# Eight gathers of 127 to 32 rows and eight single-row loads added at the turn between two graph layers

## The chip, the cores and the metric

The kernel runs on one core of a Trainium2 chip. The metric is the device time of one execution in microseconds (us); less is better. The core has a tensor engine (PE), a vector engine (DVE, VectorE), a scalar engine (ACT, ScalarE), GpSimd (POOL) and SyncE (SP). Each runs its own list of instructions, and they wait for each other on semaphores. Transfers between memory and the on-chip buffers are done by 16 DMA engines; SP, ACT and POOL issue them.

## The reference, cut to what matters

Two graph convolution layers over 6250 nodes with 128 features and 100000 edges, sorted by destination, then a layer norm over the features:

```python
def _cgconv(x, src, dst, edge_attr, Wf, bf, Ws, bs, gamma, beta, rmean, rvar):
    z = jnp.concatenate([x[dst], x[src], edge_attr], axis=-1)
    msg = jax.nn.sigmoid(z @ Wf + bf) * jax.nn.softplus(z @ Ws + bs)
    summed = jax.ops.segment_sum(msg, dst, num_segments=n)
    cnt = jax.ops.segment_sum(jnp.ones((dst.shape[0],), x.dtype), dst, num_segments=n)
    out = summed / jnp.maximum(cnt, 1.0)[:, None]
    out = (out - rmean) * jax.lax.rsqrt(rvar + BN_EPS) * gamma + beta
    return out + x
x1 = _cgconv(x, ...layer 1...)
x2 = _cgconv(x1, ...layer 2...)
return _layernorm(x + x2, axis=-1)
```

## The kernel before, in words

`graph_layer` (line 69) is built twice, for layer 1 and layer 2, and `finish` (line 846) adds up and normalises. Between the two layers all engines meet.

**Tables.** The part of z @ W that comes from x[src] is made once per node: PE multiplies the node features (held with the features in the partitions) by the source half of the weights, ACT copies the result out of PSUM (`stage_double`, line 510), and SP stores it in memory as `s_dram`, 6400 rows of 256 numbers of 4 bytes, in 13 stores of up to 512 KB (`store_s`, line 264; `store_rows`, line 200). The profile calls them s_rows. Layer 1 has its own table, s_dram1, and layer 2 has s_dram2.

**Steps.** The edges are worked in steps of 512 (4 tiles of 128 edges), 196 steps per layer, in 49 groups of 4 steps; 7 groups make the body of a loop. For each step POOL issues four indirect DMAs (`gather`, line 342), one per tile: each fetches 128 rows of the table, by the source index of each edge, into `pre`, a ring of 7 slots of 4 tiles. The indices lie in `ends`, which SP loads per group (`load_ends`, line 207). PE makes the rest of the product, DVE adds the two (line 716), ACT and DVE make sigmoid and softplus, and PE and DVE add the messages to a window of 64 nodes in `sums`. POOL may write a slot again when the softplus of the step 7 before is done (semaphore `s_soft`, line 378).

The first 7 steps of a layer are "plain": POOL gathers the node features themselves (rows of 128 numbers, from x or x1) and PE multiplies them, since the table isn't stored yet. For layer 2 these rows are in memory as `x1_rows`, which the profile calls x_rows.

**The turn.** At the start of layer 2, SP stores the edge counts and loads them in another shape, DVE inverts them, SP stores the inverses and loads them again, broadcast to 128 partitions, in five pieces (line 232). For each of five pieces DVE scales the sums (line 665) and adds them to x (line 668); that is the new x1 and raises `x_ready`. PE then turns x1 (line 415) and makes the table (line 395), ACT copies both (lines 531 and 516), and SP stores the 13 pieces of x1_rows of up to 256 KB (line 283) and the 13 pieces of the table (line 202) in an order written out by hand. Before these SP loads the edge ends of the first three groups (line 269) and the plan with the first edges (`read_plan`, line 252).

POOL's list at the turn is short: for each piece it waits for `x_ready` and clears that part of `sums` (memset, line 360), then it waits for all the stores of x1_rows (`rows_out`, line 361), then for the edge ends of group 0, and gathers. The memsets raise `zeroed`; DVE waits for all five (line 673) before it reads its column numbers and copies its first columns (line 834). In layer 2 the plain rows of x1 are staged in slots 0 to 4 of `pre` before they are stored; slots 5 and 6 are free until their first gather.

**The end of layer 1.** SP's last loop body issues the last loads of edges (line 250), then it waits for its own loads (lines 313 to 316) and for the other engines. The plan row `sp_tab`, which SP reads into registers with `entries` (line 236), holds ten numbers: the block of this row, eight window starts and the block of the next row.

Of the kernel before, what the change touches and what calls it, by code (L numbers as in the profile page):

```python
# [20 lines left out]
F2 = 2 * F  # L21
# [5 lines left out]
WIN = 64  # L27
# [20 lines left out]
NPAD = 6400  # L48
# [20 lines left out]
def graph_layer(nc, t, d, layer):  # L69
    first = layer == 1  # L70
    with nc.cleanup_on_exit(), ExitStack() as ctx:
        sb = lambda name, shape, dt: ctx.enter_context(nc.sbuf_tensor(f"{name}{layer}", shape, dt))
        ps = lambda name, shape, dt: ctx.enter_context(nc.psum_tensor(f"{name}{layer}", shape, dt))
        sem = lambda name: nc.alloc_semaphore(f"{name}{layer}")
# [3 lines left out]
        ends = sb("ends", [P, BODY, GTILES, 2], I32)  # L78
# [5 lines left out]
        pre = sb("pre", [P, RING, TILES, 3 * F], F32)  # L84
# [29 lines left out]
        ends_in, base_in = each("ends_in", BODY), each("base_in", BODY)  # L114
# [7 lines left out]
        s_gate, s_soft = each("gate_done"), each("soft_done")  # L122
        s_hot, s_msg, s_sum, s_added = each("hot_done"), each("msg_done"), each("sum_done"), each("added")
        passed = sem("waits_passed")
        if first:
            dsts_in, ends_of_pairs_in, bn_in = sem("dsts_in"), sem("ends_of_pairs_in"), sem("bn_in")
            iotas, cleared, gen_ready, filled = sem("iotas"), sem("cleared"), sem("gen_ready"), sem("filled")
            table_out = sem("table_out")
            flagged, totalled, plan, fast_ready = sem("flagged"), sem("totalled"), sem("plan_chain"), sem("fast_ready")
            split, bias_split = sem("bias_parts"), sem("bias_split")  # L130
            eps_added, rooted, bn_done, shifted = sem("eps_added"), sem("rooted"), sem("bn_done"), sem("shifted")
            dst_i = t["x1_t"][:, 0:ECOLS + 1].bitcast(I32)
            below = t["x1_t"][:, 2 * ECOLS:3 * ECOLS]
            bad = sb("bad", [P, 1], F32)
            pair_ends = sb("pair_ends", [1, 2, NPAIRS], I32)
            spans = sb("spans", [1, NPAIRS], F32)
            flag = sb("flag", [1, 4], F32)
            fast_rows = sb("fast_rows", [1, GROUPS + 2, ROW], I32)
            gen_rows = sb("gen_rows", [WINDOWS, GROUPS, ROW], I32)
            bn = sb("bn", [P, 2, 4], F32)  # L140
            root = sb("bn_root", [P, 2], F32)
        else:
            rows_turned, rows_staged, rows_out = sem("rows_turned"), sem("rows_staged"), sem("rows_out")
            cnt_out, cnt_in, inverted, inv_out = sem("cnt_out"), sem("cnt_in"), sem("inverted"), sem("inv_out")
            inv_in, scaled = each("inv_in", CHUNKS), sem("scaled")
            cnt = sb("cnt", [P, NPAD // P], F32)

        s_dram = t[f"s_dram{layer}"]
        plain_rows = d["x_rows"] if first else t["x1_rows"]
# [4 lines left out]
        def done(eng, sems, g, j, lag, each_inc=1):  # L154
            turns_back = (lag - j + SLOTS - 1) // SLOTS if lag > j else 0
            if isinstance(g, int):
                if g < turns_back:
                    return
                eng.wait_ge(sems[(j - lag) % SLOTS], (g - turns_back + 1) * each_inc)
            elif turns_back == 0:  # L160
                eng.wait_ge(sems[j - lag], g * each_inc + each_inc)
            else:
                eng.wait_ge(sems[(j - lag) % SLOTS], (g + (1 - turns_back)) * each_inc)
# [13 lines left out]
        def group_no(b, k):  # L177
            if isinstance(b, int):
                return b * BODY + k
            return b * BODY + k if k else b * BODY  # L180
# [8 lines left out]
        def n_bodies(eng):  # L189
            eng.wait_ge(planned, 1)  # L190
            return eng.value_load(t["choice"][:, 0:1], min_val=GROUPS // BODY - 1,
                                  max_val=GENERAL_GROUPS // BODY - 1) + 1

        def plain(b, k, j):
            return isinstance(b, int) and SLOTS * k + j < PLAIN

        def slot(k, j):
            return (SLOTS * k + j) % RING
# [7 lines left out]
        def _(sp):  # L206
# [69 lines left out]
            else:  # L276
                bodies, at = read_plan()
                stored = 0
                for c in range(CHUNKS):
                    for w in range(CUTS[c] // (4 * P), -(-CUTS[c + 1] // (4 * P))):  # L280
                        n = min(4, NPAD // P - 4 * w)
# [30 lines left out]
            groups = bodies * BODY  # L312
            sp.wait_ge(ends_in[0], bodies * 16 + 16)
            sp.wait_ge(base_in[0], bodies * 16 + 16)
            sp.wait_ge(sp_tab_in, groups * 16 + 16)
            sp.sem_inc(passed, 1)

        @block.gpsimd
        def _(pool):
            if first:  # L320
                nc.gpsimd.memset(fast_rows[:], 0).then_inc(cleared, 1)
                nc.gpsimd.iota(gen_rows[:, :, 0], [[1, GROUPS]], base=0, channel_multiplier=0).then_inc(gen_ready, 1)
                nc.gpsimd.iota(gen_rows[:, :, 1:ROW], [[0, GROUPS], [0, GPAIRS]], base=0, channel_multiplier=WIN
                               ).then_inc(gen_ready, 1)
                pool.wait_ge(cleared, 1)
                nc.gpsimd.iota(fast_rows[:, 0:GROUPS, 0], [[1, GROUPS]], base=0, channel_multiplier=0
                               ).then_inc(cleared, 1)
                nc.gpsimd.iota(t["lane"][:], [[1, WIN]], base=0, channel_multiplier=0,
                               allow_small_or_imprecise_dtypes=True).then_inc(iotas, 1)
                for q in range(PAIRS):  # L330
                    nc.gpsimd.iota(t["part"][:, q:q + 1], [[0, 1]], base=-WIN * q, channel_multiplier=1,
                                   allow_small_or_imprecise_dtypes=True).then_inc(iotas, 1)
                nc.gpsimd.memset(t["ident"][:], 0.0).then_inc(filled, 1)
                pool.wait_ge(filled, 1)
                nc.gpsimd.affine_select(out=t["ident"][:], in_=t["ident"][:], compare_op=ALU.not_equal, fill=1.0,
                                        base=0, pattern=[[-1, P]], channel_multiplier=1).then_inc(filled, 1)
                pool.wait_ge(filled, 2)
                pool.wait_ge(gen_ready, 2)
                pool.dma_start(table_rows[GENERAL_AT:GENERAL_AT + GENERAL_GROUPS, :].rearrange(
                    "(w b) c -> w b c", b=GROUPS), gen_rows[:]).then_inc(table_out, 16)  # L340

            def gather(rows, width, k, j):
                for i in range(TILES):
                    nc.gpsimd.indirect_dma_start(  # L344
                        pre[:, slot(k, j), i, 0:width], None, rows,
                        bass.IndirectOffsetOnAxis(ap=ends[:, k, j * TILES + i, 0:1], axis=0)
                    ).then_inc(src_in[k][j], 16)

            if first:
                pool.wait_ge(ends_in[0], 16)  # L350
                gather(plain_rows, F, 0, 0)
                pool.wait_ge(fast_ready, 1)
                pool.dma_start(table_rows[0:GROUPS + 1, :].rearrange("(a r) c -> a r c", a=1),
                               fast_rows[:, 0:GROUPS + 1, :]).then_inc(table_out, 16)
                pool.dma_start(table_rows[TABLE_ROWS - 2:TABLE_ROWS, :].rearrange("(a r) c -> a r c", a=1),
                               fast_rows[:, GROUPS:GROUPS + 2, :]).then_inc(table_out, 16)
            else:
                for c in range(CHUNKS):
                    pool.wait_ge(x_ready, c + 1)
                    nc.gpsimd.memset(t["sums"][:, 0, CUTS[c]:CUTS[c + 1]], 0.0).then_inc(zeroed, 1)  # L360
                pool.wait_ge(rows_out, 16 * QUADS)

            def one(b, k):
                g = group_no(b, k)
                if isinstance(b, int):
                    pool.wait_ge(ends_in[k], 16)
                else:
                    pool.wait_ge(ends_in[k], b * 16 + 16)
                pool.sem_inc(passed, 1)
                for j in range(SLOTS):  # L370
                    if plain(b, k, j):
                        if not (first and k == 0 and j == 0):
                            gather(plain_rows, F, k, j)
                        continue
                    if isinstance(b, int) and SLOTS * k + j == PLAIN:
                        for r in range(len(s_stage)):
                            pool.wait_ge(s_out[r], 16 * len(range(r, STORES, len(s_stage))))
                    done(pool, s_soft, g, j, RING)
                    pool.sem_inc(passed, 1)
                    gather(s_dram, F2, k, j)  # L380

            for k in range(BODY):
                one(0, k)
            bodies = n_bodies(pool)
            with pool.Fori(1, bodies) as b:
                for k in range(BODY):
                    one(b, k)
# [647 lines left out]
```

## Time and profile before

| | us |
|---|---|
| median of 3 runs | 2116.5 |
| lowest and highest | 2115.28 and 2119.24 |
| span of the profiled execution | 2110.8 |
| POOL, busy in the span | 1515.1 (72%) |
| VectorE | 1801.2 (85%) |
| ScalarE | 1677.5 (79%) |
| TensorE | 1557.2 (74%) |
| moved by DMA | 336.71 MB, 160 GB/s on the mean |

The profile is of one execution. The span runs from its first to its last instruction; the time of a run holds what lies around it as well, and the profiled execution's own run time is not given apart from the runs above. Layer 1 ends about 1025 us after the start of the span, layer 2's gathers run from 1065 to 2056 us, and the closing stage begins at about 2070 us. A row of the timeline gives the start, the duration, the engine with the line of the kernel, and in brackets how long the engine had been idle before and what ended that. SPq, POOLq and so on are an engine's sequencer, which issues DMAs. "DMA share" is the mean busy share of the 16 DMA engines; it can exceed 1 where packets of an engine overlap.

### The profile page before, as it was taken

The page shows a single profiled execution, that of the slowest core. Times are in us where ns is not written, and L with a number is a line of the kernel's source. Part 1 is how long each engine was busy: PE and PEld are TensorE (multiplying, and loading weights), DVE is VectorE, ACT ScalarE, POOL GpSimd, SP SyncE. Part 2 cuts the span into 40 slices and gives each one's busy share as a digit, 9 for nine tenths or more (in the row PEclk, how much of TensorE's full clock was granted, in tenths as well). Part 3 has the DMA queues.
Part 4 walks back from the last instruction along what each step waited for, and adds up shares of the span by engine and source line. Part 5 has one row for each costly group of instructions (what it writes and reads, how often), then busy time and mean ns, then how long its engine had stood idle before and what let it go on. Part 6 is the DMA issues. An engine that isn't in the chain of part 4 may idle for free. (4 is left out here: it accounts for less than half of the span.)

```text
span 2110.8 us, 35689 instructions
## 1 busy us (share of the span) xinstructions
PE 1557.2 (74%) x8321; PEld 1286.2 (61%) x8321; DVE 1801.2 (85%) x4354; ACT 1677.5 (79%) x2908; POOL 1515.1 (72%) x1589
## 2 busy tenths in 40 slices
PE   7777767767767787677487777777676776877773
PEld 6666656656556666566376666666565665665652
DVE  6899989989889898898549999898898887988887
ACT  5798888878878788788467888888787887887884
POOL 6677777777777777777267777777777777777770
PEclk9999999999999899999799999999999998999995
DMA  8455555555555555555475555555555555555542
GB/s 291 138 156 166 156 166 155 163 158 156 158 160 156 155 156 165 152 157 155 147 224 156 154 166 165 156 163 156 156 158 161 155 155 156 162 157 156 154 143 62
DMA packets 161806, 336.71 MB, mean 160 GB/s; under 512 B 58866, under 2 KB 85610, under 8 KB 161671
## 3 DMA queue, kind: packets, MB, share of 16 engines
q0 software_dynamic: 74496, 202.13, 32.5%
q1 hardware_dynamic: 85654, 131.58, 20.4%
q10 hardware_dynamic: 1522, 1.72, 0.3%
q14 instruction: 111, 0.91, 0.1%
q8 instruction: 23, 0.38, 0.1%
HBM read 315.49 MB, written 19.81 MB: 159 GB/s over the span
## 5 line engine op out<-in xcount | busy, mean ns | idle before, releaser
L344 POOL DMA_INDIRECT pre<-s_rows,ends x1512 | 1451.3, 960 | 473.8 <-issue 448.1
L458 PE MATMUL pre_ps<-rhs,lhs 128*128 128x256 f32 x3136 | 854.8, 417 | 463.5 <-DVE lhs L696 462.1
L458 PEld LDWEIGHTS pre_ps<-rhs,lhs 128*128 128x128 f32 x3136 | 607.0, 204 | 676.1 <-DVE lhs L696 385.0
L716 DVE TENSOR_TENSOR pre<-pre_ps,pre 128x1024 f32<-128x1024 f32 x378 | 460.7, 1219 | 52.6 <-DMA pre<-s_rows,ends 51.1
L548 ACT ACTIVATE pre<-pre 128x512 f32<-128x512 f32 x392 | 246.9, 630 | 309.3 <-DVE pre L716 270.0
L471 PEld LDWEIGHTS sum_ps<-hot,msg 128*128 128x128 f32 x3136 | 441.6, 204 | 53.2 <-issue 15.5
L696 DVE TENSOR_SCALAR lhs<-lhs,base_f,part 64x256 f32<-64x256 int32 x784 | 340.9, 435 | 114.2 <-issue 106.5
L471 PE MATMUL sum_ps<-hot,msg 128*128 128x64 f32 x3136 | 418.1, 279 | 24.8 <-DVE sums L736 24.8
L553 ACT ACTIVATE logs<-pre 128x1024 f32<-128x1024 f32 x392 | 414.3, 1057 | 12.4
L543 ACT COPY rhs<-dst_ps 64x256 f32<-64x256 f32 x792 | 290.0, 366 | 24.8 <-PE dst_ps L445 6.6
L727 DVE TENSOR_TENSOR msg<-soft_ps,logs 128x512 f32<-128x512 f32 x392 | 271.0, 691 | 13.6
L720 DVE SCALAR_TENSOR_TENSOR soft_ps<-pre,soft_ps 128x512 f32<-128x512 f32 x392 | 268.4, 685 | 2.1 <-ACT soft_ps L561 2.1
L443 PE MATMUL dst_ps<-w_node,x_cols 128*128 128x256 f32 x792 | 261.2, 412 | 8.7 <-ACT rhs L543 6.7
L559 ACT ACTIVATE logs<-logs 128x512 f32<-128x512 f32 x392 | 246.9, 630 | 12.4
L565 ACT ACTIVATE logs<-logs 128x512 f32<-128x512 f32 x392 | 240.3, 613 | 0.0
L736 DVE TENSOR_TENSOR sums<-sums,sum_ps 128x128 f32 (+1 forms) x784 | 200.4, 256 | 45.2 <-PE sum_ps L471 12.8
L561 ACT ACTIVATE soft_ps<-logs 128x512 f32<-128x512 f32 x392 | 228.3, 582 | 0.0
L753 DVE COPY x_cols<-x_t 128x64 f32 x784 | 170.6, 220 | 1.7 <-issue 1.5
L705 DVE TENSOR_TENSOR hot<-lane,rel 128x256 f32<-128x256 f32 x392 | 163.6, 417 | 0.8 <-DMA s_rows<-hot 0.8
L443 PEld LDWEIGHTS dst_ps<-w_node,x_cols 128*128 128x128 f32 x792 | 122.3, 195 | 11.0 <-issue 11.0
L445 PE MATMUL dst_ps<-bias_b,ones_b 128*128 128x256 bf16 x396 | 108.1, 273 | 0.0
L344 POOL DMA_INDIRECT pre<-x_rows,ends x56 | 53.8, 961 | 27.4 <-issue 16.5
(88 smaller groups left out, 570.8 us busy)
## 6 DMA issues: line engine op xcount, KB each, us to landing
lhs<-dge_and_destination_cols SPq DMA_DIRECT2D x196, 512.0 KB
pre<-s_rows,ends POOLq DMA_INDIRECT x1512
s_rows<-logs SPq DMA_DIRECT2D x8, 512.0 KB, 7.1
s_rows<-x_t SPq DMA_DIRECT2D x7, 512.0 KB, 10.8
s_rows<-msg SPq DMA_DIRECT2D x6, 512.0 KB, 6.1
x_rows<-pre SPq DMA_DIRECT2D x12, 256.0 KB, 4.5
out<-y_out SPq DMA_DIRECT2D x12, 256.0 KB, 2.3
ends<-edge_ends SPq DMA_DIRECT2D x100, 16.0 KB, 3.6
```

Source lines behind the costliest of these rows:

```text
L344: nc.gpsimd.indirect_dma_start(pre[:, slot(k, j), i, 0:width], None, rows, bass.IndirectOffsetOnAxis(ap=ends[:, k, j * TILES + i, 0:1], ax ...
L443: nc.tensor.matmul(dst_ps[:], x_cols[:, j].rearrange("p q w -> p (q w)"), t["w_node"][:, layer - 1, 0:F2], start=True, stop=False)
L458: ins = nc.tensor.matmul(pre_ps[:, j % 2, i, :], lhs[:, j // 2, edges], rhs[:, j, i // 2, :], start=True, stop=not plain(b, k, j))
L471: ins = nc.tensor.matmul(sum_ps[:, q, 0, 0:WIN], msg[:, j, 2 * q + i, :], hot[:, j, 2 * q + i, :], start=i == 0, stop=i == 1)
L543: ins = nc.scalar.copy(rhs[hot_rows[q], j, q, :], dst_ps[hot_rows[q], :])
L548: nc.scalar.activation(pre[:, at, :, F2:3 * F], pre[:, at, :, F:F2], ACT.Abs).then_inc(s_abs[j], 1)
L553: nc.scalar.activation(logs[:, j % 2].rearrange("p k (h f) -> p k h f", f=F), pre[:, at].rearrange("p k (h f) -> p k h f", f=F)[:, :, 0:3: ...
L559: nc.scalar.activation(logs[:, j % 2, :, 0:F], logs[:, j % 2, :, 0:F], ACT.Ln, bias=1.0).then_inc(s_log_f[j], 1)
L696: ins = nc.vector.tensor_scalar(lhs[hot_rows[q], j // 2, at], lhs[hot_rows[q], j // 2, at].bitcast(I32), base_f[hot_rows[q], k, PAIRS * j ...
L716: nc.vector.tensor_tensor(rows, pre_ps[:, j % 2], rows, ALU.add).then_inc(s_pre[j], 1)
L720: nc.vector.scalar_tensor_tensor(soft_ps[:, j % 2], pre[:, at, :, F:F2], 0.0, soft_ps[:, j % 2], ALU.max, ALU.add).then_inc(s_soft[j], 1)
L727: nc.vector.tensor_tensor(msg[:, j], soft_ps[:, j % 2], logs[:, j % 2, :, 0:F], ALU.mult).then_inc(s_msg[j], 1)
```

## The change

At the end of layer 1, SP waits for one more semaphore, reads eight window starts of the last plan row into registers, loads the eight rows of the table s_dram1 that they name, one DMA each, into partition 0 to 7 of slot 0 of `pre`, and waits for them. At the start of layer 2, before its memsets, POOL waits for the edge ends of group 0, gathers 127, 126, 125, 124, 120, 96, 64 and 32 rows (814 in all, 1 KB each) of layer 1's table into slots 5 and 6 of `pre`, and waits for all of them. Nothing reads what either part brings; later gathers overwrite it.

```diff
@@ -144,6 +144,7 @@
             cnt = sb("cnt", [P, NPAD // P], F32)
+            odd_in = sem("odd_in")
@@ -314,6 +315,13 @@
             sp.wait_ge(sp_tab_in, groups * 16 + 16)
             sp.sem_inc(passed, 1)
+            if first:
+                sp.wait_ge(s_soft[1], groups + (-1))
+                sp.sem_inc(passed, 1)
+                rows = entries(1, 8, NPAD - WIN)
+                for i in range(8):
+                    sp.dma_start(pre[i:i + 1, 0, 0, 0:F2], s_dram[bass.ds(rows[i], 1), :]).then_inc(bn_in, 16)
+                sp.wait_ge(bn_in, 16 * 9)
@@ -355,6 +363,12 @@
             else:
+                pool.wait_ge(ends_in[0], 16)
+                for i, n in enumerate((127, 126, 125, 124, 120, 96, 64, 32)):
+                    nc.gpsimd.indirect_dma_start(
+                        pre[0:n, 5 + i // 4, i % 4, 0:F2], None, t["s_dram1"],
+                        bass.IndirectOffsetOnAxis(ap=ends[0:n, 0, i, 0:1], axis=0)).then_inc(odd_in, 16)
+                pool.wait_ge(odd_in, 16 * 8)
                 for c in range(CHUNKS):
                     pool.wait_ge(x_ready, c + 1)
                     nc.gpsimd.memset(t["sums"][:, 0, CUTS[c]:CUTS[c + 1]], 0.0).then_inc(zeroed, 1)
```

## Rows read from the trace of the kernel before

**Rows 1.** The page: busy time of each engine, and the software queue's packets, MB, share.

```profile
PE 1557.2 (74%) x8321; PEld 1286.2 (61%) x8321; DVE 1801.2 (85%) x4354; ACT 1677.5 (79%) x2908; POOL 1515.1 (72%) x1589
...
q0 software_dynamic: 74496, 202.13, 32.5%
```

**Rows 2.** Waits of POOL, whole span: us in total, times, longest.

```profile
POOL pre L344 <- issue: 464.5, 1523, 0.6
```

**Rows 3.** Groups of POOL's instructions, 1101 to 2060 us: busy, mean ns, idle before.

```profile
L344 POOL DMA_INDIRECT pre<-s_rows,ends x756 | 725.3, 959 | 230.4 <-issue 223.0 <-DVE soft_ps L720 7.3
```

**Rows 4.** Timeline of POOL at the turn: start us, us, what, idle before.

```profile
1011.25 0.94 POOL L344 DMA_INDIRECT pre<-s_rows,ends  x1 [0.30 <-issue]
1039.63 0.53 POOL L360 MEMSET sums<- 128x512 f32 x1 [27.44 <-DVE x_t L668]
1042.10 0.95 POOL L360 MEMSET sums<- 128x1024 f32 x1 [1.94 <-DVE x_t L668]
1045.62 1.38 POOL L360 MEMSET sums<- 128x1536 f32 x1 [2.57 <-DVE x_t L668]
...
1053.20 1.59 POOL L360 MEMSET sums<- 128x1792 f32 x1 [2.68 <-DVE x_t L668]
1065.47 0.95 POOL L344 DMA_INDIRECT pre<-x_rows,ends  x1 [10.68 <-DMA x_rows<-pre]
```

**Rows 5.** Timeline of POOL: a gather early in layer 1, and the last of layer 2.

```profile
55.48 2.34 POOL L344 DMA_INDIRECT pre<-s_rows,ends  x1 [0.30 <-issue]
...
2055.05 0.95 POOL L344 DMA_INDIRECT pre<-s_rows,ends  x1 [0.30 <-issue]
```

**Rows 6.** Timeline of VectorE: the last rows that wait for a gather, layer 1 and 2.

```profile
1015.35 1.23 DVE L716 TENSOR_TENSOR pre<-pre_ps,pre 128x1024 f32<-128x1024 f32 x1 [2.56 <-DMA pre<-s_rows,ends]
...
2059.19 1.23 DVE L716 TENSOR_TENSOR pre<-pre_ps,pre 128x1024 f32<-128x1024 f32 x1 [2.67 <-DMA pre<-s_rows,ends]
```

**Rows 7.** Instructions of pre, 1040 to 1070 us: the stores of x1_rows, ns min/median/max.

```profile
L283 SPq DMA_DIRECT2D x_rows<-pre x13: 441/885/2113, 1042.9 to 1061.3; - x13
...
DMA to landing us min/median/max: 3.4/4.5/9.7
```

**Rows 8.** Instructions of out, 2060 us to the end: the stores of the result.

```profile
L871 SPq DMA_DIRECT2D out<-y_out x12: 372/372/399, 2081.9 to 2106.2; - x12
...
DMA to landing us min/median/max: 2.3/2.3/2.6
```

**Rows 9.** Stages of the turn: busy (count) of PE, PEld, DVE, ACT, POOL; clock, DMA, GB/s.

```profile
1037.00:1045.00 8.00, 5.37 (x19) 4.65 (x20) 6.80 (x6) 2.34 (x4) 1.48 (x2) 0.50 1.00 379
1045.00:1048.00 3.00, 2.67 (x18) 1.98 (x17) 2.96 (x3) 2.02 (x4) 1.38 (x1) 0.99 0.09 11
...
1050.00:1065.00 15.00, 13.32 (x70) 11.18 (x68) 5.08 (x14) 9.86 (x18) 2.11 (x2) 1.00 1.09 346
```

**Rows 10.** Timeline of VectorE at the turn: first columns, and first turned tile.

```profile
1057.32 1.00 DVE L834 COPY x_cols<-x_t 128x64 f32 x8 [4.18 <-issue]
...
1078.90 0.69 DVE L748 COPY pre<-pre_ps 128x512 f32<-128x512 f32 x1 [17.78 <-PE pre_ps L437]
```

**Rows 11.** End of layer 1: softplus, SP's last load, its wait, its register loads.

```profile
991.23 0.69 DVE L720 SCALAR_TENSOR_TENSOR soft_ps<-pre,soft_ps 128x512 f32<-128x512 f32 x1
...
992.41 0.33 SPq L250 DMA_DIRECT2D lhs<-dge_and_destination_cols  x1
...
SPq L71 <- PEq L71: 33.1, 2, 31.7
...
L237 SPq TENSOR_LOAD <-sp_tab x2: 274/352/431, 971.8 to 972.2; - x2
```

**Rows 12.** Instructions of ends, 1034 to 1042 us: the loads of the edge ends.

```profile
L208 SPq DMA_DIRECT2D ends<-edge_ends x3: 432/433/486, 1037.1 to 1038.1; - x3
...
DMA to landing us min/median/max: 8.4/8.4/8.4
```

**Rows 13.** The stage with the most GB/s at the turn, columns as in rows 9.

```profile
1042.00:1044.00 2.00, 2.00 (x11) 1.91 (x10) 1.97 (x3) 1.17 (x2) 0.95 (x1) 0.50 1.04 434
```

## The prediction

> **What bounds the kernel now.** I read the page first. GpSimd (POOL) is busy only 72% of the span, VectorE 85% [rows 1], but the table of waits says what the idle part is: 464.5 us in 1523 pieces of at most 0.6 us that no other engine ends [rows 2]. So the gaps belong to the gather itself. Nothing else held POOL back in layer 2: from 1101 to 2060 us it has 756 gathers, 725.3 us busy and 230.4 us of gaps, and a gap laid to VectorE is the same 0.30 us as the others (7.3 us in all) [rows 3]. One gather therefore costs POOL 0.95 + 0.30 = 1.25 us, and layer 2 is one unbroken row of 784 of them, from 1065.47 to 2056.00 us [rows 4, 5]. VectorE adds the last gathered rows at 2059.19, about 3 us behind [rows 6], and the closing stage follows. **The time of layer 2 is set by the moment at which POOL starts its first gather; each us that this slips is a us at the end.** What happens elsewhere at the turn counts only if it moves that start.
>
> What releases that start: POOL sat idle 10.68 us before it, until the stores of the x1 rows had landed (DMA x_rows<-pre) [rows 4]. Those 13 stores are issued by SyncE between 1042.9 and 1061.3 and land 3.4 to 9.7 us later [rows 7]. A store of the same 256 KB costs 0.37 us to issue at the end of the kernel and lands in 2.3 us [rows 8]; here the medians are 0.885 and 4.5 us. SyncE is held back by full queues. The stages agree: the DMA engines are filled from 1037 to 1045 (share 1.00), almost idle from 1045 to 1048 (0.09), and filled again from 1050 to 1065 (1.09) [rows 9]. So the bound at the turn is the traffic on the 16 DMA engines after 1048 us.
>
> A second path is nearly as tight. The tables' stores (s_rows) share those queues, the table copies wait on them, and VectorE's first turned tile comes at 1078.90 after an idle 17.78 us [rows 10]. Their later work is paced by the same DMA engines, so it moves with the first path.
>
> **The change, part by part.**
>
> **SyncE at the end of layer 1.** The wait asks for the second last group's slot 1, whose softplus runs at 991.23 to 991.92, before SyncE's last load of edges at 992.41: it is no wait. Behind it SyncE waits 31.7 us for the other engines to end the layer [rows 11]. Eight register loads at 0.27 to 0.43 us are 2.8 us; eight issues at 0.34 us, with up to 0.2 us of register work each, are 4.3 us; the landing, by the nearest rows, is 2.3 to 9.7 us [rows 7, 8]. That ends 9 to 17 us after 992.8, with 31.7 us of cover. It moves 8 KB. Nothing is queued behind it on SyncE but the end of the layer. Cost 0; without the cover it would be the full 10 us.
>
> **GpSimd's wait for the edge ends at the turn.** They are issued at 1037.08 and land 8.4 us later, behind the five broadcasts of the inverses: POOL can begin at 1045.5 [rows 12]. Before the change it was then in its third memset.
>
> **Eight gathers.** Issue: 8 x 1.25 = 10.0 us, so to 1055.5 [rows 4]. I take the price of a full gather; fewer rows may be cheaper (bound: 0.3 us each, 2.4 us) or dearer (layer 1 has one of 2.34 us, right after the tables' stores [rows 5]; 8 x 2.64 = 21 us). Landing: the last gather of layer 1 starts at 1011.25 and VectorE uses it at 1015.35, 4.1 us later [rows 4, 6]. So the wait on all eight ends at about 1054.3 + 4.1 = 1058.4 on free queues.
>
> **The five memsets behind that wait.** They were spread from 1039.63 to 1054.79, each behind VectorE. Now they run together: 0.53 + 0.95 + 1.38 + 1.38 + 1.59 = 5.83 us, so to 1064.2 [rows 4] (two of the five are 1536 columns wide and have one duration). VectorE waits for them before it loads its first columns: 9.4 us later than before, at about 1067 instead of 1057.32. Its next work that hangs on a transfer comes at 1078.90, behind an idle 17.78 us, half of which is left [rows 10]: covered. POOL's next gather could start at 1064.2 + 0.3; it starts at 1065.47 today. **POOL's own path has 1 us of slack.**
>
> **The gathered bytes.** 814 rows of 1 KB. The software queue moved 202.13 MB in 32.5% of 16 engines' span, 10,976 us, or 55.6 ns for a KB [rows 1]. No row shows a gather of fewer than 128 rows. The packets say how a full one is cut: 74496 over 1568 gathers is 47.5, close to 3 for each of 16 engines, thus 8 rows each. Bounds for the new ones: spread evenly, 814/16 = 51 rows, 2.8 us for every engine. Cut into equal shares, the only cut the trace shows, 127 rows go to one engine alone, 126 to 14 (9 each), 125 to 5 (25), 124 to 4 (31), 120 to 15 (8), and 96, 64, 32 to all (6, 4, 2). One engine then has 147 to 172 rows: 8.2 to 9.6 us. I take equal shares, because they are what 1568 gathers did, and 170 rows, 9.4 us.
>
> By the Trainium skill, "DMA: Bandwidth & Descriptors", section "Why a DMA increments its semaphore by 16 and not by 1", the engine count is the largest up to 16 that divides the rows, 127 partitions falling on one; the same section tells of direct software copies on trn2 that use 16 engines with unequal shares, which would give the 2.8 us. No gather in this trace tells the two apart.
>
> These rows start moving at about 1047. The idle stretch to 1048 and the start of the filled one take some 1.3 us of them; in the filled stretch the share is 1.09, so overlapping packets may hide another 1.5 to 2 us. The rest, 9.4 - 1.3 - 2 = **6 us**, comes on top of the stores' part on that engine, and a store has landed only when its slowest engine is done. From 1050 on the engines are full until after the last of these stores is issued [rows 7, 9], so nothing later takes the 6 us up. If the engine serves the two queues turn by turn, the stores slip less but the gathers last longer: 8.1 us at half speed is 16 us, to 1064, and the memsets behind that end at 1070, plus 0.3: 5 us late. Both ways the first gather comes at about 1071.
>
> **Sum:** 0 (SyncE) + 0 (issue and memsets, with 1 us of slack) + 6 (start of POOL's row) = +6 us. Against the profiled execution: span 2110.8 to 2116.8. The median of the runs, 2116.5, lies 5.7 us above that span (start and end outside it, and spread of the runs); I add the 6 us to it: **2122.5 us**. A measurement of this kernel can tell about 0.2% from no change, 4.2 us.
>
> **Rivals.**
> - *Even spread (22%).* 2.8 us more on every engine, of which the idle stretch takes 1: start 2 us late, 2118.5. For it: nothing forbids unequal shares. Against: all gathers seen have equal ones.
> - *Hidden (13%), the not-slower side.* Place: the stores' queues from 1048 to 1061. If memory and not the DMA engines limits the stores, the slow engine has spare time: a DMA engine moves 21.6 GB/s (346/16) there [rows 9], but 27.1 (434/16) at its best, from 1042 to 1044 [rows 13]. A fifth of 17 us is 3.4 us; with the gap's 1.3 that covers 4.7 us. It decides where the engine's extra work is under 4.7 us and the gathers land before 1059.3 (1065.47 less 6.1). Then 2116.5. Against: share over 1 throughout, and back pressure on SyncE.
> - *POOL's own path (7%).* If odd gathers cost 2.34 + 0.3 us to issue, or POOL must wait for room, they end at 1067, the wait at 1069.5, the memsets at 1075.3: 10 us late, 2126.5. It decides once a gather takes over 1.4 us.
> - *A slight gain (3%).* The memsets no longer run beside VectorE's steps on the sums, which may end sooner. No row shows a step drawn out by a memset; I give this up to 4 us, down to 2112, and little faith. That the change does not act is no case of its own: both parts stand outside any branch on data.
>
> **How the numbers follow.** Forecast 55%, with its own range 2120 to 2126 (8.2 us less all cover, 3.5; 9.6 us nearly uncovered, 9); about a fifth of it lies under 4.2 us. Slower: 0.55 x 0.82 + 0.07 + a little of the even spread = 0.53. Faster: 0.04, from the last rival and noise. Same: 0.43. The range, 2117 to 2126.5, takes in the even spread and the forecast, and leaves out most of the hidden case and the far end.
>
> **What would show it.** In the changed trace: eight gathers from s_rows at 1045.5 to 1055.5 at 1.25 us; the five memsets in one block ending at 1064 to 1070; the first gather from x_rows at about 1071, released by the DMA of x_rows or directly by the memsets; then 784 gathers in 990 us without a wait. The eight single rows between 993 and 1003. It is wrong if the first gather still starts by 1067, or if POOL shows new waits for VectorE later in layer 2.

## The result and the profile after

The changed kernel takes 2124.44 us at the median of 4 runs (2124.13 to 2127.03), the kernel before 2115.89 (2114.08 to 2119.24, now 4 runs). The ratio is 1.0041, with a 95% interval of 1.0029 to 1.0052: slower by 8.6 us, where 6 had been forecast. The profiled execution of the changed kernel took 2124.51 us, with a span of 2122.7 us.

That span is 11.9 us longer than the profiled one of before, and a third of it is not the change's. To part the two I take in every trace the start of layer 1's last gather as zero. It stands at 1011.25 us before [rows 4] and at 1015.23 after. The 4.0 us between them arise in the first 60 us of layer 1, where nothing was changed, and the traces of both kinds of kernel differ there (it stands between 1011.47 and 1016.69 in the others). The profiled execution of before was simply an early one: with the 1.8 us that lie around the span after, it would be a run of 2112.6, below all four runs above.

From that zero, in us:

| | before | after |
|---|---|---|
| VectorE's first piece of x1 (L668, L682) begins | 27.6 | 27.4 |
| last store of the x1 rows issued by | 50.9 | 56.5 |
| POOL's five memsets end | 43.5 | 58.6 |
| POOL's first gather from x_rows | 54.2 | 60.8 |
| POOL's last gather of layer 2 | 1043.8 | 1051.3 |

So 6.6 us are lost at the turn, and 1.0 us in the 990 us after it. The lines of the timeline of POOL after, which answer to [rows 4]:

```profile
1015.23 0.95 POOL L352 DMA_INDIRECT pre<-s_rows,ends  x1 [0.30 <-issue]
1050.05 3.65 POOL L368 DMA_INDIRECT pre<-s_rows,ends  x1 [33.87 <-DMA ends<-edge_ends]
1054.00 1.90 POOL L368 DMA_INDIRECT pre<-s_rows,ends  x1 [0.30 <-issue]
1056.20 2.03 POOL L368 DMA_INDIRECT pre<-s_rows,ends  x1 [0.30 <-issue]
1058.54 1.29 POOL L368 DMA_INDIRECT pre<-s_rows,ends  x1 [0.30 <-issue]
1060.14 0.97 POOL L368 DMA_INDIRECT pre<-s_rows,ends  x1 [0.30 <-issue]
...
1063.87 0.87 POOL L368 DMA_INDIRECT pre<-s_rows,ends  x1 [0.30 <-issue]
1068.29 5.58 POOL L374 MEMSET sums<- 128x512 f32 x5 [3.54 <-DMA pre<-s_rows,ends]
1076.02 0.96 POOL L352 DMA_INDIRECT pre<-x_rows,ends  x1 [2.15 <-DMA x_rows<-pre]
```

POOL starts its gathers when the edge ends have landed, needs 14.7 us to issue the eight, waits 3.54 us for them, clears for 5.58 us, and then still waits 2.15 us for the stores of the x1 rows. It is the stores that release it.

The stages of the turn after, columns as in [rows 9]; the first stage stands 4 us later than there:

```profile
1041.00:1049.00 8.00, 5.56 (x20) 4.46 (x20) 6.86 (x6) 2.35 (x4) 0.00 (x0) 0.54 1.00 378
1049.00:1052.00 3.00, 2.29 (x16) 1.84 (x16) 2.96 (x3) 2.00 (x4) 1.95 (x1) 1.00 0.09 11
1052.00:1060.00 8.00, 5.66 (x37) 4.19 (x36) 5.12 (x3) 4.92 (x10) 6.92 (x4) 1.00 1.07 341
1060.00:1067.00 7.00, 7.00 (x34) 6.17 (x33) 0.00 (x0) 4.12 (x9) 3.69 (x4) 1.00 0.73 209
1067.00:1075.00 8.00, 4.58 (x18) 3.63 (x17) 0.00 (x0) 1.64 (x4) 5.58 (x5) 0.83 1.01 306
```

The fourth row is the new thing: in the middle of the stretch that had been full, the DMA engines drop to a share of 0.73 and 209 GB/s, though SyncE has stores to issue. The timeline of SyncE's sequencer after shows it standing in them: six stores take 12.84 us. The last line is the one of before that answers to them.

```profile
1050.43 4.04 SPq L203 DMA_DIRECT2D s_rows<-logs  x1
1054.51 12.84 SPq L284 DMA_DIRECT2D x_rows<-pre  x6
1067.40 0.76 SPq L203 DMA_DIRECT2D s_rows<-logs  x1
1068.20 3.55 SPq L284 DMA_DIRECT2D x_rows<-pre  x4
...
1050.32 6.65 SPq L283 DMA_DIRECT2D x_rows<-pre  x6
```

Before, the same six took 6.65 us. DMA engines stand idle while SyncE cannot go on, which suggests that one of them, or a few, are behind. The trace also records the single packets, and their sizes say how the gathers were cut. Up to four rows of 1 KB go in one packet (the eight full gathers of experiment e3, below, are 256 packets of 4 KB). With that, equal shares of the 814 rows make 179 packets of 4 KB, 5 of 3 KB, 32 of 2 KB and 19 of 1 KB, and the software queue has exactly these at the turn. Shares of 8 rows with a smaller last one would give the 126 rows no packet of 1 KB, the 125 one and not five, and the 124 none of 3 KB and not four, so that cut is ruled out for these three. For 127 rows both cuts give the same sizes; experiment e5 tells them apart by time.

SyncE's own part, at the end of layer 1 (its timeline, and its waits from 990 to 1040 us), answers to [rows 11]:

```profile
1000.09 3.16 SPq L323 DMA_DIRECT2D pre<-s_rows  x8
...
SPq L71 <- PEq L71: 26.2, 2, 24.7
...
SPq L71 <- DMA pre<-s_rows: 1.3, 1, 1.3
```

The eight rows are issued in 3.16 us and have landed after 1.3 us more; then SyncE waits 24.7 us for the others. In layer 2 POOL has 767 gaps of at most 0.3 us laid to its own issue and no wait over 0.3 us but the first.

### The profile page after: what moved, and what is told of

It reads as the page before. It is cut to its first block and busy times, and to the rows that moved or that the text cites. A ratio compares the mean times of both kernels' runs of the same rounds, so it can differ in the third digit from the quotient of the medians.

```text
span 2122.7 us, 35726 instructions
## 1 busy us (share of the span) xinstructions
PE 1572.3 (74%) x8321; PEld 1297.1 (61%) x8321; DVE 1800.8 (85%) x4354; ACT 1678.0 (79%) x2908; POOL 1530.4 (72%) x1597
```

## The experiments

The theory: the cost is the eight gathers; rows that 16 doesn't divide fall in equal shares on fewer DMA engines, 127 of them on one, and the stores of the x1 rows wait for that engine. The rivals: the bytes as such; POOL's own path (gathers, landing, memsets); SyncE's single rows. The twelve kernels were run in three groups, each beside the kernel before on the same chip; its median there was 2116.31 (e1 to e4), 2116.24 (e5 to e8) and 2115.95 us (e9 to e12). "Late" is how much later than before POOL's first gather from x_rows comes, counted from the zero above. The times of one kernel spread over up to 8 us. "Late" is the sharper number, though it comes from one trace of each kernel: the three kernels with the same turn (the changed one, e1 and e4) have 6.6, 6.6 and 6.5 us, and e2, with the turn of before, has -0.1.

**The two parts alone.** e1 takes SyncE's part out, e2 the gathers.

```diff
e1:
-            if first:
-                sp.wait_ge(s_soft[1], groups + (-1))
...
-                sp.wait_ge(bn_in, 16 * 9)
e2:
-                pool.wait_ge(ends_in[0], 16)
-                for i, n in enumerate((127, 126, 125, 124, 120, 96, 64, 32)):
...
-                pool.wait_ge(odd_in, 16 * 8)
```

> The changed kernel without SyncE's eight single-row loads; the eight gathers of 127 to 32 rows stay. Theory (the gathers at the turn are the whole cost): 2124 to 2125 us, as the changed kernel (2124.4), and the first gather from x_rows starts some 7 us later after the end of layer 1's gathers than before. Rival (the single-row loads cost part of it, by holding SyncE or the end of layer 1): 2116 to 2121 us.

Measured: 2121.88 us, ratio 1.0030 (1.0018 to 1.0042); 6.6 us late. The median lies under what was expected, between theory and rival; the trace is that of the changed kernel.

> The changed kernel without the eight gathers; SyncE's single-row loads stay. Theory: 2116 us, as before (2115.9), with the single rows landed 20 us before the layer ends. Rival: over 2118 us.

Measured: 2117.04 us, ratio 1.0005 (0.9996 to 1.0014); 0.1 us early. SyncE's part costs nothing that can be seen; by the interval it is under 3.0 us. The gathers are the cost.

**Bytes or spread.** e3 makes all eight gathers full.

```diff
-                for i, n in enumerate((127, 126, 125, 124, 120, 96, 64, 32)):
+                for i, n in enumerate((128,) * 8):
```

> Eight gathers of 128 rows in place of those of 127 to 32: 1024 rows, 26% more bytes, but each spread evenly over the 16 DMA engines. Theory (a gather whose rows 16 doesn't divide falls on few engines, dear to issue and slow to land, and holds up SyncE's stores): each is issued in 0.95 us, the stores slip by 2 to 3 us (1024/16 rows x 47 to 56 ns less the idle gap), 2117 to 2120 us. Rival 1 (the bytes cost, however spread): 2125 to 2127 us. Rival 2 (POOL's own path: wait for the ends, eight gathers, memsets): issue ends at 10 us, memsets near 1064 on the clock of the trace before, so at most 1 to 2 us late, 2117 us.

Measured: 2122.28 us, ratio 1.0034 (1.0024 to 1.0044); 4.4 us late. The median lies above the theory and the second rival and below the first rival, and the trace shows none of the three pictures whole. The stores were issued 1.9 us later than before (52.8 us after zero), as the theory had it; but POOL did not wait for them. It started 0.16 us after its memsets. Timeline of POOL of e3:

```profile
1051.48 1.99 POOL L368 DMA_INDIRECT pre<-s_rows,ends  x1 [34.62 <-DMA ends<-edge_ends]
1053.77 1.55 POOL L368 DMA_INDIRECT pre<-s_rows,ends  x1 [0.30 <-issue]
1055.63 1.62 POOL L368 DMA_INDIRECT pre<-s_rows,ends  x1 [0.30 <-issue]
1057.56 1.82 POOL L368 DMA_INDIRECT pre<-s_rows,ends  x1 [0.30 <-issue]
1059.68 0.94 POOL L368 DMA_INDIRECT pre<-s_rows,ends  x1 [0.30 <-issue]
...
1068.73 5.59 POOL L374 MEMSET sums<- 128x512 f32 x5 [4.36 <-DMA pre<-s_rows,ends]
```

Two things were wrong in my account of POOL's own path. The first four gathers cost 1.55 to 1.99 us and not 0.95, and the landing after the last takes 4.4 us. The ends land 1.3 us later than in the trace before (35.6 us after zero, for 34.3). All this together makes the path end 4.4 us too late by itself, where I had given it 1 us of slack.

**Which of the two releases POOL.** e4 moves the wait for the gathers behind the wait for the stores.

```diff
-                pool.wait_ge(odd_in, 16 * 8)
                 for c in range(CHUNKS):
                     pool.wait_ge(x_ready, c + 1)
...
                 pool.wait_ge(rows_out, 16 * QUADS)
+                pool.wait_ge(odd_in, 16 * 8)
```

> The changed kernel, but POOL waits for the eight gathers only behind its wait for the x1 rows' stores, so the memsets don't wait for their landing (3.5 us in the changed kernel's trace). Theory (the stores, held up on one DMA engine, release POOL's first gather; it waited 2.15 us for them after the memsets): no gain, 2124 to 2125 us. Rival (POOL's own path decides): 2121 to 2122 us, 2 to 3.5 us less.

Measured: 2126.03 us, ratio 1.0044 (1.0032 to 1.0056); 6.5 us late. The memsets begin 3.6 us sooner after zero, and POOL's wait for the stores grows from 2.15 to 5.66 us. No gain: in the changed kernel the stores decide. Row of POOL's timeline of e4:

```profile
1075.87 0.96 POOL L352 DMA_INDIRECT pre<-x_rows,ends  x1 [5.66 <-DMA x_rows<-pre]
```

**The gather of 127 rows.** e5 keeps it alone, e6 keeps the other seven.

```diff
e5:
+                for i, n in enumerate((127,)):
...
+                pool.wait_ge(odd_in, 16)
e6:
+                for i, n in enumerate((126, 125, 124, 120, 96, 64, 32)):
...
+                pool.wait_ge(odd_in, 16 * 7)
```

> The changed kernel with one gather, of 127 rows, in place of the eight. Theory (its rows lie on one DMA engine, 127 x 47 to 56 ns = 6 to 7 us of it, and the stores wait for that engine): the stores of the x1 rows still slip by 3.5 to 5 us of the 5.6 that they slip with all eight, 2119.5 to 2121 us. Rival (the rows are spread, or the bytes of all gathers cost): under 1 us, 2116 to 2117 us.

Measured: 2120.6 us, ratio 1.0026 (1.0017 to 1.0035); 4.4 us late, with the stores issued 3.7 us late. One gather of 127 KB makes two thirds of what the turn loses. Timeline of POOL, the stage of the lag and one us of it, e5:

```profile
1050.44 3.55 POOL L368 DMA_INDIRECT pre<-s_rows,ends  x1 [33.73 <-DMA ends<-edge_ends]
1063.71 5.59 POOL L374 MEMSET sums<- 128x512 f32 x5 [9.73 <-DMA pre<-s_rows,ends]
1074.41 0.97 POOL L352 DMA_INDIRECT pre<-x_rows,ends  x1 [5.11 <-DMA x_rows<-pre]
...
1060.00:1067.00 7.00, 7.00 (x34) 6.15 (x34) 0.00 (x0) 4.78 (x10) 3.29 (x4) 1.00 0.63 184
...
1063.00:1064.00 1.00, 1.00 (x6) 0.87 (x6) 0.00 (x0) 0.58 (x1) 0.29 (x1) 1.00 0.06 23
```

It lands 9.73 us after its issue has ended, where the last gather of layer 1 was used 3.16 us after (1012.19 to 1015.35, [rows 4, 6]). The packets say why: they begin 3.5 us after that, and the 127 rows move in 32 packets, one after another and never two at once, from 1057.50 to 1063.22 us. That is one engine for 5.7 us, or 45 ns for a row. The last line shows what this does to the stores. Just behind the gather, the share of all 16 engines is 0.06, one sixteenth: a single engine is working off what it still owes, and nothing else moves, although SyncE is in the middle of its six stores (11.63 us for them here).

> The changed kernel without the gather of 127 rows; the seven of 126 to 32 stay, 687 rows. Theory: the fullest DMA engine has 50 to 80 rows, so the stores slip by 1 to 2.5 us; the gathers end earlier by the 4 us that the first one costs to issue. 2117 to 2119 us. Rival (POOL's own path decides, with the memsets behind the gathers): their issue of 9 to 11 us, landing 3.5 us and memsets 5.6 us end at about where the first gather stood before, 2116.5 to 2118 us. If it is still over 2120 us, the gather of 127 rows isn't the main cost.

Measured: 2118.97 us, ratio 1.0012 (1.0003 to 1.0021); 2.3 us late, the stores 0.8 us. POOL again starts 0.16 us after its memsets: here its own path decides, as the rival had it, and the stores slip less than the theory's 1 to 2.5 us. The path is longer than the rival had it, so that the median lies 1 us above its range.

**How the rows are cut.** e7 issues eight gathers of 127 rows.

```diff
+                for i, n in enumerate((127,) * 8):
```

> Eight gathers of 127 rows. Theory (one gather of 127 rows lies on one DMA engine, the next on the engine after it): each gather costs POOL more to issue than a full one, and eight engines hold 127 rows each rather than one, so the stores slip by 6 to 9 us, little more than in the changed kernel, since the engines work side by side. If all eight fell on the same engine, it would hold 1016 rows, 50 us. Issue: if the 3.65 us of the first gather are a price of 127 rows, POOL needs 8 x 3.9 = 32 us for the eight and its first gather slips by over 20 us; if they are a price of the first gather or of the work beside it, only 4 to 8 us.

Measured in a single run: 2150.97 us; 31.7 us late. Timeline of POOL of e7:

```profile
1051.22 3.60 POOL L368 DMA_INDIRECT pre<-s_rows,ends  x1 [35.02 <-DMA ends<-edge_ends]
1055.13 3.46 POOL L368 DMA_INDIRECT pre<-s_rows,ends  x1 [0.30 <-issue]
1058.90 2.54 POOL L368 DMA_INDIRECT pre<-s_rows,ends  x1 [0.30 <-issue]
...
1070.27 2.54 POOL L368 DMA_INDIRECT pre<-s_rows,ends  x1 [0.30 <-issue]
1083.11 2.54 POOL L368 DMA_INDIRECT pre<-s_rows,ends  x1 [10.30 <-issue]
1095.39 5.58 POOL L374 MEMSET sums<- 128x512 f32 x5 [9.74 <-DMA pre<-s_rows,ends]
```

127 rows cost POOL 2.54 us to issue, each time, and about 1 us more in the first two. Seven could be issued; before the eighth POOL stood for 10.30 us. It issued the eighth at 1083.11, when the rows of the first seven had all moved (at 1082.02 by the packets). I take this for a lack of room, but the trace names no releaser, so that stays open. The stores' issue ended 10.8 us late, somewhat more than the 6 to 9 expected. Up to four packets of the gathers move at once, where the single gather of e5 never had two, so by this the gathers fall on at least four different engines.

**The same gathers in a quieter place.** e8 lets SyncE load the ends before the counts' round trip.

```diff
                 sp.dma_start(cnt_row, t["sums"][0:1, 1, :]).then_inc(cnt_out, 16)
+                for k in range(EARLY):
+                    load_ends(k, k)
...
-            for k in range(1 if first else 0, EARLY):
+            for k in range(1, EARLY) if first else ():
                 load_ends(k, k)
```

> The changed kernel, but SyncE loads the edge ends of the first three groups before the round trip of the counts, so that POOL begins its eight gathers some 15 us earlier, while VectorE is idle and the DMA engines mostly are. Theory (the gathers cost because they meet the stores of the x1 rows and tables on the DMA engines): the stores no longer slip on their account; what is left is that the broadcasts of the inverses meet the gather of 127 rows, 0 to 3 us. 2115 to 2119 us. Rival (POOL's work itself costs, wherever it stands): 2122 us or more. Beside it: if the dear issues (3.65, 1.90, 2.03 us) come from VectorE's long steps on the sums, they fall to about 1 us here; if they belong to the row counts, they stay.

Measured: 2123.23 us, ratio 1.0038 (1.0025 to 1.0052); 5.8 us late. The time is the rival's, the cause is not. POOL is through with gathers and memsets early and waits 10.47 us for the stores; these come late because x1 does. VectorE begins its first piece of x1 33.1 us after zero instead of 27.4, for SyncE waited 5.5 us for its store of the inverses, 25 KB, which takes 1.1 us otherwise. That store is 128 packets of 200 bytes. In e8, 120 of them have begun by 1037.07 us and the last 8, one engine's equal share, follow 0.17 to 0.18 us apart from 1038.80 to 1040.03. A 4 KB packet of a gather takes 0.16 us, so one of them fits between each two. Timeline of POOL, and SyncE's waits, of e8:

```profile
1031.78 2.57 POOL L370 DMA_INDIRECT pre<-s_rows,ends  x1 [18.11 <-DMA ends<-edge_ends]
1034.66 0.99 POOL L370 DMA_INDIRECT pre<-s_rows,ends  x1 [0.30 <-issue]
1035.95 1.21 POOL L370 DMA_INDIRECT pre<-s_rows,ends  x1 [0.30 <-issue]
1037.47 1.29 POOL L370 DMA_INDIRECT pre<-s_rows,ends  x1 [0.31 <-issue]
1039.07 0.97 POOL L370 DMA_INDIRECT pre<-s_rows,ends  x1 [0.30 <-issue]
...
1042.80 0.87 POOL L370 DMA_INDIRECT pre<-s_rows,ends  x1 [0.30 <-issue]
1072.77 0.96 POOL L354 DMA_INDIRECT pre<-x_rows,ends  x1 [10.47 <-DMA x_rows<-pre]
...
SPq L235 <- DMA node_inverses<-cnt: 5.5, 1, 5.5
```

I had looked at the mean share of the DMA engines and called the stretch quiet. The chain there is one of short transfers that wait for each other, and one laggard engine delays each of them. So e8 doesn't test the gathers in a quiet place; it moves what they delay from the stores of the x1 rows to the inverses.

These rows also give the clean price of each gather, since VectorE had only 1 us of work beside them, on the counts. If the rows are cut into equal shares, 127, 124, 125, 126 and 120 rows put 127, 31, 25, 9 and 8 rows on a DMA engine, and 32 rows put 2. The prices are 2.57, 1.29, 1.21, 0.99, 0.97 and 0.87 us: between 127 and 8 rows 1.60 us for 119 rows, 13.4 ns for a row, and by that 31, 25 and 9 rows come to 1.28, 1.20 and 0.98. 124 rows cost more than 125 and these more than 126, which the count of rows cannot explain and the equal shares do. It is the rule of the Trainium skill, "DMA: Bandwidth & Descriptors", section "Why a DMA increments its semaphore by 16 and not by 1": the number of engines is the largest up to 16 that divides the rows. Its exception for direct copies does not show in these indirect ones.

**One row more.** e9 makes the first gather 128 rows and leaves the rest.

```diff
+                for i, n in enumerate((128, 126, 125, 124, 120, 96, 64, 32)):
```

> The changed kernel with its first gather widened from 127 to 128 rows: one row more, the other seven as they are. Theory (the 127 rows lie on one DMA engine and hold the x1 rows' stores up by 3.7 us in the run with that gather alone; the other seven hold them by 0.8): the stores slip by 1 to 1.5 us only, the first gather is issued in about 2.0 us instead of 3.6, and POOL's own path (gathers, landing, memsets) becomes the bound, as in the run with eight full gathers: the first gather from x_rows 3.5 to 4.5 us late instead of 6.6, 2119 to 2121 us. Rival (rows count, not their spread): no change, 6.6 us late, 2122 to 2124 us.

Measured: 2120.98 us, ratio 1.0022 (1.0012 to 1.0032); 3.5 us late, the stores 1.2 us, the first gather issued in 2.08 us, POOL released by its memsets. With one row more to fetch, the turn is 3.1 us shorter than in the changed kernel, as the theory had it; the medians, each against its own median of before, say 3.5 us.

**A version that beats both?** Three orders of the kernel before. e10 stores the x1 rows before the table, e11 loads the ends and window starts of three groups on ScalarE's queue during the counts' round trip, e12 does both.

```diff
e10:
-                    while c < CHUNKS - 1 and 2 * stored + 2 <= c + 1:
-                        store_s(stored)
-                        stored += 1
e11 (on ScalarE, in layer 2; taken out of SyncE's list):
+                for k in range(EARLY):
+                    act.dma_start(ends[:, k, :, :], ...).then_inc(ends_in[k], 16)
...
+                for k in range(EARLY):
+                    act.dma_start(base_i[:, k, :], ...).then_inc(base_in[k], 16)
```

> The kernel before, with one order changed: SyncE stores all thirteen pieces of the x1 rows before the first pieces of the table, which came between them. Theory (POOL's start waits for the landing of the x1 rows behind everything in SyncE's queue): POOL starts 2 to 3 us earlier, since two stores of 512 KB no longer stand in front; but the table's stores and with them the first product come no earlier, and step 11 had only 0.8 us of slack, so POOL gives most of it back as a wait for VectorE. 2114 to 2116 us. Rival (the second path has room): 2113 to 2114 us.

Measured: 2116.96 us, ratio 1.0010 (1.0001 to 1.0019). POOL started 2.9 us earlier after zero and gave it all back, and 1.6 us more, waiting for VectorE's softplus. Timeline of POOL of e10:

```profile
1063.07 0.95 POOL L341 DMA_INDIRECT pre<-x_rows,ends  x1 [7.85 <-DMA x_rows<-pre]
...
1114.33 1.09 POOL L341 DMA_INDIRECT pre<-s_rows,ends  x1 [1.38 <-DVE soft_ps L717]
...
1123.12 1.09 POOL L341 DMA_INDIRECT pre<-s_rows,ends  x1 [3.84 <-DVE soft_ps L717]
```

> The kernel before, but the edge ends and window starts of the first three groups of layer 2 are loaded by ScalarE's queue while the counts make their round trip, not by SyncE between the inverses and the x1 rows. Theory (the idle stretch of the DMA engines at 1045 to 1048 comes from the small broadcast loads that stand in SyncE's queue in front of the x1 rows' stores; both paths wait on that queue): the stretch goes, stores and tables come 2 to 4 us earlier, 2112 to 2114 us. Rival (the stretch is a wait for VectorE's x1): within 0.5 us of before.

Measured: 2116.98 us, ratio 1.0006 (0.9997 to 1.0015). The idle stretch is gone, but x1 comes 1.9 us later (29.5 us after zero), since the new loads stand beside the inverses: SyncE stood 3.9 us from its store of them to their first load (1032.71 to 1036.59), and 1.5 us before. POOL starts 1.1 us earlier, its last gather 0.9 us: nothing that the runs can tell.

> The two last edits together on the kernel before: early loads on ScalarE's queue, and the x1 rows stored before the table. Theory: POOL starts 4 to 6 us earlier; the table's path comes 2 to 4 us earlier and now decides, so the gain is about that of the early loads alone, up to 1 us more: 2111 to 2113 us. If the order alone gained nothing and this gains no more than the early loads, the second path is the bound.

Measured: 2115.53 us, ratio 1.0002 (0.9993 to 1.0011). POOL starts 3.4 us earlier and its last gather comes as before. All three missed what I expected by 1 to 3 us, and no version beat the kernel before. The reason stands in the trace of before, where VectorE's softplus of step 5 ends 0.78 us before POOL takes its slot again, at step 12 (timelines of VectorE and POOL):

```profile
1124.35 0.69 DVE L720 SCALAR_TENSOR_TENSOR soft_ps<-pre,soft_ps 128x512 f32<-128x512 f32 x1
...
1125.82 1.09 POOL L344 DMA_INDIRECT pre<-s_rows,ends  x1 [0.36 <-issue]
```

POOL cannot come much earlier unless VectorE does, and none of the three brought VectorE forward: its first turned tile comes 69.3, 69.0 and 68.9 us after zero in e10, e11 and e12, and came 67.7 before (1078.90 less 1011.25, [rows 4, 10]). I take the stores of the table for what holds it, but no run was made to show that.

## Why the prediction was right

The sign, the place and most of the size were right: 8.6 us (6.1 to 11.0 by the interval) against 6, with 2126.5 as the upper end. By its own steps:

- **POOL's start sets the end.** Right. 6.6 us late at the first gather, 7.5 us at the last one, without a wait between. In e6 and e9 the last gather is late by 4.5 and 3.9 us, the first by 2.3 and 3.5. Where POOL hardly waits for VectorE, the row of 784 gathers takes 989 to 992 us, so the shift is kept only within 2 or 3 us.
- **SyncE's part is free.** Right, by e2: 3.2 us of issue for the 4.3 counted, and 24.7 us of cover left.
- **POOL can begin when the ends land.** Right, 34.8 us after zero for the 34.3 counted.
- **Equal shares; 127 rows on one engine.** Right, and the step on which the forecast hung. The sizes of the packets, the 32 packets in a row in e5, the issue prices of e8 and the pair e5 and e9 show it.
- **The stores slip by 6 us.** They were issued 5.6 us late. The agreement is partly luck. It was 9.4 us of one engine less two covers that I had guessed. A row took 45 ns on its engine in e5, not 55.6, so the 170 rows would be 7.7 us, and less the same covers 4.4. The bounds of 147 to 172 rows don't follow from the shares either: these alone allow 139 to 212 rows on the engine that has the 127. The runs give 3.7 us for the gather of 127 rows alone, 0.8 for the other seven alone, and 5.6 for all eight.
- **POOL's own path has 1 us of slack.** Wrong. The issue took 14.7 us, not 10.0, and the memsets end at 58.6 us after zero, 4.4 us later than the first gather stood before. I had the price of a full gather among VectorE's steps of layer 2, and took it for any gather beside any work. The error did not show in the sum because the stores were later still (e4), but it is why full gathers in their place (e3) are not cheap.
- **The two ways to 6 us.** I had said that either the stores or the gathers would be late, at about 1071. Both were, and the stores decided.
- **The rivals.** The even spread is ruled out by the packets and by e5 and e9, and the hidden case by the stores, which slipped. POOL's own path was to decide once a gather takes over 1.4 us. They took 1.84 us on the mean, gaps included, and yet the path ended 4.4 us late and not 10, behind the stores: the dear issues were few. The slight gain didn't come: VectorE's ten steps on the sums take 15.0 us before and 15.3 after.

The rest between 6.6 us at the turn and 8.6 us in the medians: 1.0 us is in the gathers of layer 2. The other us stays open; the three kernels with this turn (the changed one, e1 and e4) have medians of 2124.44, 2121.88 and 2126.03 us, so it is within what their runs spread.

## What to carry to other kernels

Give a gather a count of rows that the 16 DMA engines can share, even if some rows are fetched for nothing: 128 rows instead of 127 took 3 us off a turn of 61. A lull in the mean DMA share isn't free time: every transfer waits for its slowest engine, and in e8 a store of 25 KB took 5.5 us for 1.1. When two paths meet at a start, moving work off one of them pays only as far as the other's slack, here about 0.8 us: POOL started up to 3.4 us earlier in e10 and e12 and nothing was gained.

## What the runs showed of the hardware

- **The issue of a gather has a price by the fullest DMA engine**, 0.87 us with 2 rows on it to 2.57 us with 127, 13.4 ns a row (e8, e7). The rows themselves took 45 ns each on that engine (e5).
- **One engine can hold up all the others' work.** In e5 a full us passes in which one engine of 16 moves data, at 23 GB/s, while SyncE has stores to issue.
- **VectorE's steps on the sums stretch it.** In e3 a full gather costs 1.55 to 1.99 us while VectorE works with two operands in the on-chip buffer, and 0.94 us after the last of these, which begins at 1056.47 us and takes 2.08:

```profile
1054.42 2.02 DVE L679 TENSOR_TENSOR sums<-sums 128x1792 f32<-128x1792 f32 x1
1056.47 2.08 DVE L682 SCALAR_TENSOR_TENSOR x_t<-sums,bn_scale,x_t 128x1792 f32<-128x1792 f32 x1
```

  The same goes for the changed kernel (3.65, 1.90 and 2.03 us beside them; 2.57, 0.99 and 1.21 in e8 without). In layer 2's steps, where VectorE is as busy but its long steps take one operand from PSUM (L716, L720), a gather keeps to 0.95 us, and the memsets, which only write, took 5.6 us together or 5.8 spread out among the steps on the sums. The Trainium skill, "SBUF — State Buffer", section "Who interferes with whom", says it so: a VectorE instruction with two inputs in the on-chip buffer contends with a GpSimd instruction that reads it, not with one that only writes. The runs agree; none was made to part the kinds of VectorE's operands.
- **POOL can stand before a gather without a named reason**: 10.30 us before the eighth of 127 rows (e7). The wait ended 1.1 us after the rows of the first seven had moved.
